# Projections by token tiles, and five token groups in front of the experts: one change to a fused encoder kernel

## The reference

```python
h  = patches(x) @ W.T + b + pos                       # 36 rows a sequence
ht = gelu(tok_embed[x_txt] @ W1.T + b1) @ W2.T + b2   # 32 rows a sequence
h  = concatenate([h, ht], axis=1)
y  = layernorm(h) @ fq_weight(w_qkv).T + b_qkv        # then fq_act: needs min and max of all of y
attn = int_log_softmax(fq_act(q @ k.T * hd**-0.5)); o = fq_act(attn @ v)
h  = h + fq_act(o @ fq_weight(w_proj).T + b_proj)
x2 = layernorm(h)
scores = sigmoid(x2 @ router_w.T); idx = top_k(scores + balance_bias, 2)
h  = h + mlp_shared(x2) + sum over the 2 experts of weight * mlp_expert(x2)   # mlp: square(relu(x@w1))@w2, 8 experts
```

## Time and profile before

| what | us |
|---|---|
| median of 3 runs | 1002.32 |
| the profiled execution's own time | 1000.82 |
| its span, first to last instruction | 999.0 |
| TensorE busy / VectorE busy | 623.0 / 724.1 |
| ScalarE busy / GpSimd busy | 512.8 / 325.4 |
| mean granted TensorE clock, share of full | 0.694 |

### The profile page before, as it was taken

The page is one execution under the profiler, slowest core; times in us unless marked ns, Lnnn a source line. Parts: engine busy times, 40 slices in busy tenths (PEclk is TensorE's granted clock), DMA queues, the critical chain, the costliest instruction groups (busy, mean ns, idle before and its releaser), DMA issues.

```text
span 999.0 us, 20044 instructions
## 1 busy us (share of the span) xinstructions
PE 623.0 (62%) x6502; PEld 472.7 (47%) x6502; DVE 724.1 (72%) x1719; ACT 512.8 (51%) x898; POOL 325.4 (33%) x347
## 2 busy tenths in 40 slices
PE   3599688586543377604888888734222357998950
PEld 2599577475432244402555555423122246776740
DVE  3435554767577599967999999999888754657773
ACT  3122276453531844233888888843644225887820
POOL 2022355444333121001232222220046770025575
PEclk9999698897867555555556555555555587999985
DMA  7963044221101344302222222272111323567653
GB/s 182 255 178 100 12 121 120 58 59 40 59 21 39 81 109 116 85 0 52 33 42 42 45 42 41 26 221 89 52 44 67 127 88 85 154 176 219 188 141 103
DMA packets 155152, 92.76 MB, mean 93 GB/s; under 512 B 88488, under 2 KB 147696, under 8 KB 154960
## 3 DMA queue, kind: packets, MB, share of 16 engines
q1 hardware_dynamic: 147232, 72.28, 28.0%
q0 software_dynamic: 7856, 19.68, 6.8%
HBM read 45.62 MB, written 31.85 MB: 78 GB/s over the span
## 4 chain that ended last, share of the span: by engine, by line
DVE 22%; PE 21%; issue 18%; SPq 15%; POOL 14%; ACT 5%; DMA 4%; POOLq 1%; DVEq 0%; ACTq 0%
PE ps L1702 16%; SPq L591 7%; POOL x_by_expert L752 5%; POOL R L761 3%; ACT R L768 3%; POOL R L695 2%; DVE M L1285 2%; DVE M L1286 2%; SPq L566 2%; SPq L565 2%; SPq L567 2%; POOL R L686 1%; PE ps L1969 1%; POOL R L684 1%; DVE R L1275 1%
## 5 line engine op out<-in xcount | busy, mean ns | idle before, releaser
L1702 PE MATMUL ps<-R 128*128 128x256 f16 (+6 forms) x2024 | 304.6, 307 | 48.2 <-DVE R L1659 12.9
L1702 PEld LDWEIGHTS ps<-R 128*128 128x128 f16 (+3 forms) x2024 | 222.5, 132 | 102.1 <-issue 52.4
L768 ACT ACTIVATE R<-ps 128x768 f16<-128x768 f16 (+7 forms) x257 | 178.1, 730 | 101.6 <-PE ps L1969 36.0
L1702 PE MATMUL ps<-M 32*128 32x68 bf16 (+4 forms) x1192 | 101.6, 245 | 101.7 <-DMA M<-R 69.4
L1702 PEld LDWEIGHTS ps<-M 32*128 32x128 bf16 (+3 forms) x1192 | 65.7, 116 | 153.7 <-issue 61.2
L771 ACT ACTIVATE R<-R,sc 128x512 f16<-128x512 f32 (+11 forms) x107 | 83.8, 839 | 101.9 <-DMA R<-v_rows 28.0
L768 ACT ACTIVATE R<-R 128x512 f16<-128x512 f32 (+5 forms) x145 | 74.7, 533 | 105.8 <-POOL R L686 66.6
L733 POOL TENSOR_TENSOR R<-R,M 128x884 f32<-128x884 f32 x32 | 53.2, 1664 | 147.7 <-ACT M L912 147.7
L761 POOL DMA_INDIRECT R<-y_by_tile,M x68 | 67.0, 986 | 101.0 <-DMA y_by_tile<-R 82.1
L752 POOL DMA_INDIRECT x_by_expert<-R,M x68 | 67.2, 988 | 59.7 <-DVEq L1578 39.5
L1873 PE MATMUL ps<-ident_b,R 128*68 128x128 bf16 x416 | 56.2, 308 | 20.9 <-ACT R L768 19.0
(11 more groups left out here) (279 smaller groups left out, 1130.9 us busy)
## 6 DMA issues: line engine op xcount, KB each, us to landing
R<-x_by_expert SPq DMA_DIRECT2D x41, 192.0 KB, 2.9
y_by_tile<-R SPq DMA_DIRECT2D x41, 192.0 KB, 2.6
R<-in_x_dram SPq DMA_DIRECT2D x12, 576.0 KB, 8.4
M<-R SPq DMA_DIRECT2D x16, 260.0 KB, 3.1
M<-R SPq DMA_DIRECT2D x32, 130.0 KB, 2.0
R<-w_split SPq DMA_DIRECT2D x1, 4032.0 KB, 22.7
v_rows<-R SPq DMA_DIRECT2D x16, 204.0 KB
R<-v_rows SPq DMA_DIRECT2D x16, 204.0 KB
```

Of the source, the lines that this page charges most:

```text
L768: return act.activation(out_, in_, ACT.Copy)
L1702: return pe.matmul(o, a, b, start=start, stop=stop, skip_group_check=True)
```

## The change

**Projection.** The columns of `xT` are ordered by tile, so `x_out` writes them one behind the other. `qkv` takes units of tiles instead of sequences: 8 of text (2 tiles, 256 columns) and 8 of images (3 tiles, 288 columns), at the steps of `UNITS_AT`: text units at 2 to 7, 24 and 26, image units at 10, 11, 16, 17, 22, 23, 25 and 28. There are 30 steps. `evac_qk` and `extremes_qkv` of an image unit reach into the sequence order by runs of 3 values with steps of 6, and `evac_qk` reads the bank with a step of 96 values. Normalising moves to ScalarE (`normal`, one instruction), the bias of V becomes one more matmul with three rows for each tile (`ones_three`, `bv_three`, prepared by `v_ratio`), the maximum of V is taken while it is scaled, all three channels of `by_patch` are on GpSimd, six buffers instead of four hold normalised tiles, and `turn_x` follows one step behind `x_low`.

**V.** The 16 loads become 4 of 816 KB, issued by ScalarE ahead of `to_halves`.

**Experts.** Five groups; `READY` becomes 11, 19, 29, 37, 41. ScalarE normalises (two Identity instructions for a pair) in `x2_high`. Square roots become Ln and Exp, the sigmoid an Exp with an addition and a reciprocal on VectorE. `weigh` (the weights of the copies) is split from `choose` and put later. 12 shared units stand ahead of the routed ones. `combine` is spaced by 2 steps.

```diff
-WINDOWS = [(0, 5), (5, 12), (12, 17)]
-SHARED_FIRST = 10
+WINDOWS = [(0, 2), (2, 6), (6, 11), (11, 15), (15, 17)]
+SHARED_FIRST = 12
-        XSTEP = [k // 2 for k in range(16)] + [6 * q + 8 + w // 2 for q in range(3) for w in range(6)] + [23, 23, 24, 26, 26, 26]
-        GSTEP = [11, 12, 14, 15, 17, 18, 20, 21, 23, 24, 25, 26, 27, 28, 29, 30]
+        XSTEP = [k // 2 for k in range(16)] + [6 * q + 8 + w // 3 for q in range(3) for w in range(6)] + [23, 23, 23, 26, 26, 26]
+        UNITS_AT = {2: 0, 3: 1, 4: 2, 5: 3, 6: 4, 7: 5, 10: 8, 11: 9, 16: 10, 17: 11, 22: 12, 23: 13, 24: 6, 25: 14, 26: 7, 28: 15}
-        WSTEP = [6, 7, 13, 16, 19, 22]
+        WSTEP = [9, 12, 13, 18, 19, 21]
...
-                pool.tensor_tensor(v, h, mv[0:n, x, 0:1].to_broadcast([n, C]), ALU.subtract).then_inc(sem("centred"), 1)
-                pool.tensor_tensor(v, v, rs[0:n, 2, x:x + 1].to_broadcast([n, C]), ALU.mult).then_inc(sem("xn"), 1)
-                pool.tensor_tensor(v, v, bvrow[0:N, :].unsqueeze(1).to_broadcast([N, 4, C]), ALU.add).then_inc(sem("v_stored"), 1)
+                ident_(xf1[0:n, x % XR1], h, scale=rs[0:n, 2, x:x + 1], bias=rs[0:n, 0, x:x + 1]).then_inc(sem("xn"), 1)
...
-                    copy(to, o.rearrange("p (k b h) -> p k b h", k=3, h=GRID)).then_inc(sem("xT"), 1)
+                copy(xT[:, :, x_cols(x)], ps[:, 4, :].bitcast(F16)[:, at:at + 3 * n].rearrange("p (k t) -> p k t", k=3)).then_inc(sem("xT"), 1)
...
+                        y = y[:, 16 * q:16 * q + 16, 0:NI].rearrange("p b (h w) -> p b h w", w=GRID)[:, :, :, 3 * half:3 * half + 3]
+                        o = o[:, 0:288].rearrange("p (w b h) -> p b h w", w=3, h=GRID)
...
             barrier(act, "act")
+            for q in range(4):
+                act.dma_start(yv[:, 16 * q:16 * q + 16, :], v_dram[16 * q:16 * q + 16].rearrange("b n c -> n b c")).then_inc(sem("v_in"), 16)
-            act.wait_ge(sem("v_in"), 16 * 16)
+            act.wait_ge(sem("v_in"), 16 * 4)
...
-                act.activation(rs2[:, 1, t], rs2[:, 0, t], ACT.Sqrt).then_inc(sem("ln2_sqrt"), 1)
+                chain(act, "scalar_step", act.activation(rs2[:, 1, t], rs2[:, 0, t], ACT.Ln))
+                act.activation(rs2[:, 1, t], rs2[:, 1, t], ACT.Exp, scale=0.5).then_inc(sem("ln2_sqrt"), 1)
...
+                act.wait_ge(sem("ln2_done"), window_of(i) + 1)
+                wait(act, "rows2", i - 1)
+                for j in range(2):
+                    n = 2 * i + j
+                    last = ident_(xf[:, i % 2, j, :], hf[:, n, :], scale=rs2[:, 2, n:n + 1], bias=rs2[:, 0, n:n + 1])
+                chain(act, "scalar_step", last)
...
-                        if s > GSTEP[0]:
-                            extremes_qkv(GSTEP.index(s) - 1)
-                        scale_v(GSTEP.index(s))
+                if s - 1 in UNITS_AT:
+                    extremes_qkv(UNIT_ORDER.index(UNITS_AT[s - 1]))
+                if s in UNITS_AT:
+                    scale_v(UNIT_ORDER.index(UNITS_AT[s]))
...
+                        mm(o, both, wqT1[:, 2 * C:3 * C], False, False)
+                        last = mm(o, ones_three[:, 0:m], bv_three, False, True)
...
+            def beside(low, more):
+                for k in range(max(len(low), len(more))):
+                    if k < len(more):
+                        residual(more[k])
+                    if k < len(low):
+                        x2_low(low[k])
+                    if k < len(more):
+                        stats(more[k])
...
+            beside([], [0, 1])
             variances(0)
             deviations(0)
+            beside([0, 1], [2, 3])
             choose(0)
+            beside([], [4])
             place(0)
+            beside([], [5])
             variances(1)
             deviations(1)
+            beside([2, 3, 4, 5], [6, 7, 8])
             choose(1)
...
+            beside([15, 16], [])
+            weigh(2)
+            weigh(3)
+            choose(4)
+            place(4)
             make_table()
+            weigh(4)
             y_rows()
```

More of the change, by code:

```diff
@@ L969, in x2_out, with exponentials @@
                      ps[:, 4 + i % 2, :].bitcast(F16)[:, 0:6 * P].rearrange("p (k t) -> p k t", k=3)).then_inc(sem("X"), 1)
-            def sigmoids(w):
+            def exponentials(w):
                 t = WBLK[w]
                 act.wait_ge(sem("routed"), WINDOWS[w][1])
-                act.activation(scores[:, t, :], ps[:, 6, t.start * E:t.stop * E].rearrange("p (i e) -> p i e", e=E), ACT.Sigmoid, scale=s1(W_RU)).then_inc(sem("sigmoid"), 1)
-            def x2_window(w):
-                first, end = WINDOWS[w]
-                for i in range(first, end + 1):
-                    if i < end:
-                        x2_high(i)
-                    if i > first:
-                        x2_out(i - 1)
@@ L984, in _ @@
-            for i in range(8):
+                act.activation(scores[:, t, :], ps[:, 6, t.start * E:t.stop * E].rearrange("p (i e) -> p i e", e=E), ACT.Exp, scale=s1(W_RU)).then_inc(sem("sigmoid"), 1)
+            for i in range(5):
                 y_whole(i)
             roots(0)
+            x2_high(0)
+            x2_high(1)
+            x2_out(0)
+            y_whole(5)
+            x2_out(1)
+            exponentials(0)
+            y_whole(6)
+            y_whole(7)
+            roots(1)
@@ L987, in _ @@
+            x2_high(2)
             y_whole(8)
+            x2_high(3)
+            x2_out(2)
             y_whole(9)
-            x2_window(0)
-            sigmoids(0)
-            for i in range(10, 14):
-                y_whole(i)
-            roots(1)
-            y_whole(14)
+            x2_high(4)
+            x2_out(3)
+            x2_high(5)
+            x2_out(4)
+            x2_out(5)
+            exponentials(1)
+            for i in range(10, 13):
+                y_whole(i)
+            roots(2)
@@ L1225, in _ @@
             ln_deviation(0)
-            for s in range(STEPS):
+            ch(dve.memset(ext, 0.0))
+            for s in range(STEPS + 1):
                 if s >= 1 and s - 1 in LN_STEP:
@@ L1512, in deviations @@
                 ch(ts(rs2[:, 2, t], rs2[:, 2, t], X_UNIT, None, ALU.mult))
-            def normal(i):
-                wait(dve, "rows2", i - 1)
-                for j in range(2):
-                    n = 2 * i + j
-                    last = ts(xf[:, i % 2, j, :], hf[:, n, :], mv2[:, n, 0:1], rs2[:, 2, n:n + 1], ALU.subtract, ALU.mult)
-                last.then_inc(sem("xf"), 1)
+                ch(dve.scalar_tensor_tensor(rs2[:, 0, t], rs2[:, 2, t], -1.0, mv2[:, t, 0], ALU.mult, ALU.mult))
+                dve.drain().then_inc(sem("ln2_done"), 1)
             def x2_low(i):
@@ L1558, in choose, with weigh @@
                 tt(mask[:, t, :], at[:, :, 0, :], at[:, :, 1, :], ALU.add).then_inc(sem("mask"), 1)
+            def weigh(w):
+                t = WBLK[w]
+                n = t.stop - t.start
+                s, at, got = scores[:, t, :], chosen[:, t], picked[:, 0:n]
                 ch(tt(got, at, s.unsqueeze(2).to_broadcast([P, n, TOP, E]), ALU.mult))
@@ L1594, in make_table @@
                     ch(tt(cum[:, b, n:NQE], cum[:, a, n:NQE], cum[:, a, 0:NQE - n], ALU.add))
-                ends = cum[:, 1, :]
-                ch(dve.scalar_tensor_tensor(start_row, full[:, 0:3, :], float(TILE), own, ALU.mult, ALU.add))
+                ends = cum[:, 0, :]
+                ch(dve.scalar_tensor_tensor(start_row, full[:, 0:NW, :], float(TILE), own, ALU.mult, ALU.add))
                 ch(tt(tiles, ends, tiles, ALU.subtract))
@@ L1954, in turn_window @@
                         route(i - 2)
-            for w in range(3):
+            for w in range(NW):
                 turn_window(w)
```

424 lines of the change are left out of this document (242 added, 182 removed).

## The result

The changed kernel took 970.49 us (median of 4, 964.69 to 976.77) where before took 1001.39 beside it: ratio 0.969, interval 0.962 to 0.976. The forecast was 945, its range 921 to 983. The profiled execution has a span of 974.8 us, 24.2 less than before's 999.0 and 32 more than the sum. It was the slowest of the four (976.77), so its trace shows 24 of the 31 us that the medians show.

The account below looks back on a forecast made before the run. A ring of waits, with no engine full, was taken to bound the projection stage. From the span of 999.0, -52 (projection) -1.2 (V) +8.7 (prelude) -11.7 (tail) gave 942.8; with 1.8 outside the span, 945 us, range 921 to 983.

Parts of the forecast that it names:

- forecast case: Whole kernel: all terms come as summed, 945 us, own range 930 to 962; chance 0.55.
- The third case: Projection's evacuations and reductions: steps cost 3.6 ns a value everywhere, +28 us, time 973; chance 0.16.
- the fourth case: Projection: the ring closes again elsewhere, in ScalarE's in-order stream; the stage saves 25 instead of 52, time 972; chance 0.09.
- the V term: V's loads: issuing four costs ScalarE 5.5 us, VectorE's 6.65 us wait goes; -1.2 us, between -5.5 and +3.
- Projection, -52: Projection stage of 206.5 us: with the ring open it ends near 266 instead of 318 us, saving 52.
- The ring: Projection: GpSimd's normalising and V bias and VectorE's scaling and `x_low` wait in a circle; GpSimd waits 83.2 us for scaling.
- 13 in additions: Projection: 5 us for image evacuations and 8 us for parts at the low clock, on top of 141.4 for steps.
- The 5 us for the evacuations: Projection: evacuating an image unit's Q and K takes 0.9 us; about 5 us of the excess is in the way.
- Its own sign of being wrong: V's loads: the prediction would be wrong if ScalarE's issues of V took over 8 us.
- Prelude and shared units, +8.7: Experts: first routed tile comes 10.5 us later, behind 12 shared units, 1.8 comes back; +8.7, between +2 and +14.
- Tail, -11.7: First routed tile to end: third group starts two tiles sooner, 157.8 us instead of 169.5; between -4 and -14.
- The slower case: Projection: TensorE stays at 1.2 GHz, its 101 us become about 203, stage ends at 340, time 1019; chance 0.06.

Follow-up runs that it names:

- the four cases of GpSimd: Changed kernel, V's loads back on SyncE, with neither, normalising, V's bias or both back on GpSimd: ratios 0.9423, 0.938, 0.939, 0.9735.
- v_act_16: Changed kernel with V loaded by 16 DMAs from ScalarE at the same place instead of four of 816 KB: 1047.85 us, ratio 0.9716.
- v_on_sp: Changed kernel with V's loads put back as 16 DMAs of 204 KB issued by SyncE: 1017.18 us, ratio 0.9423.
- v_mid: Changed kernel with V's 16 loads on SyncE behind groups 0 to 13, two behind groups 6 and 10: 928.98 us, ratio 0.9292.

## Why the prediction was right in sign and off by half in size

The time of 970.49 us lies in the range of 921 to 983, but not in the forecast case's own 930 to 962. Near it stood only the third and the fourth case (973 and 972), for which the range had been widened, and neither happened. That the range held is luck: the miss came from the V term, which none of the cases had.

- **Projection, -52, measured -58.3, by itself -61.6.** The ring was the right diagnosis, shown by the four cases of GpSimd: it needs both pieces. But it was half of the gain, and the text spoke as if it were the whole. The stage's work ended at 263.1 (266 forecast), 151.6 us in place of 141.4 for the steps and 13 in additions. That the sum came so near is in part luck too. The 5 us for the evacuations had no ground (646 ns, not 0.9 us); what the low clock cost is not separated from the rest (granted 0.88, up from 0.81); and two steps of 8.8 and 8.9 us, where TensorE waits behind a batch of deviations, put in some 11 us that the sum didn't have. VectorE's work came to 112.9, the upper end. Another 3.5 us, not foreseen, are the scales: VectorE waited 4.1 us for GpSimd's reduction there, now 0.6.
- **The third case (steps cost 3.6 ns a value everywhere).** It did not happen. The rule of the Trainium skill ("Advanced Engine Details and Errata", section "Memory Cachelines") holds in this case for `x_out`, 1273 ns with steps of 12 bytes and 407 in order. Of its statement on the bank little shows here: a read with 384 bytes from value to value ran at 646 ns for 288, beside 576 for 256 and 583 for 272 in order. The prediction also misread its runs of 3 by that rule: with a step of 24 bytes from run to run, every second run has one value alone in its line. The reductions ran as in order all the same.
- **V, -1.2 between -5.5 and +3, measured +33.8: the failed step.** The prediction took 5.5 us for issuing four loads, and 8.5 as the upper end, from "0.47 for one large issue and 8.00 for the one behind it, blocked". It read the blocked 8.00 as one price for the whole set; it was the price behind each load. And it took it from a load of 128 partitions, which all 16 engines carry, for loads of 68, which four carry: 0.27 against 1.02 of the engines, 48 us instead of some 10. The row was the nearest at hand, and it differed in what mattered. (The bound of +3 is not what its working gives either: 8.5 less 6.7 is 1.8.) Its own sign of being wrong, issues of V at over 8 us, came out at 34.8. The 16 issues of before took 0.3 us each though such loads are as slow in transfer (0.27 of the engines in `v_act_16`), since they stood 5 us apart with other work between them. In place of the step stand 34.8 us of issue and 7.3 us of late Q and K, less 6.65 and 1.7 us of VectorE's waits that went: 33.8. Undone, it gives back 34.0.
- **Prelude and shared units, +8.7, measured +12.3 and +1.0 ahead of it.** The working held to 1.6 us at every scatter. The first routed tile is 2 us later than the sum (818.25; 839.75 - 23.6 = 816). The 1.8 us that the prediction gave back for before's start on cold tiles lie behind that tile (its second comes 4.35 us later before, 2.27 after), so the two rows are better held against +10.5 and -13.5 than against +8.7 and -11.7.
- **Tail, -11.7, measured -13.0** (156.6 us; 157.8 forecast). Right also in its mechanism: the third group's gathers begin 94 us behind the first routed tile and run through.
- **The slower case and the fourth** did not happen: the clock rose, and ScalarE waited at most 14 us for any one line. The slower case was also priced a little high: 101 us by its own rows (4.05 against 2.12) become 193, not 203.

## What to carry to other kernels

In these runs an issue of a DMA was cheap (0.3 to 0.8 us) with nothing large ahead of it, and cost up to 13.5 us behind a slow load: price it by the transfer ahead of it, and read the share of the DMA engines, which shows when a load leaves most of them idle (0.27 for 68 partitions, 1.02 for 128). Such loads belong between other work, not in a block on a queue that the path needs. A ring of waits can need two edges in one stream: try each alone before crediting either, and ask how much of the gain the ring holds. Where a stage is opened, sum the fullest engine's work by steps, and in the steps with a batch of small operations on another engine ask who waits for them: that was the 11 us which the sum lacked.

## Not expected

The queue's price does not depend on the engine (ScalarE 34.8 us, SyncE 46 with the fourth load's), and a single load of 3264 KB costs its issuer 0.52 us. What V would cost as two loads, of 64 and of 4 partitions, was not tried. On the first chip (`v_on_sp`) VectorE's chained small operations at the end of the prelude stood 1.40 us apart:

```profile
780.76 0.20 DVE L1697 TENSOR_TENSOR R<-R 128x40 f32<-128x40 f32 x1 [1.20 <-DVE R L1696]
782.16 0.20 DVE L1698 SCALAR_TENSOR_TENSOR R<-R 128x40 f32<-128x40 f32 x1 [1.20 <-DVE R L1697]
```

where in `v_mid`, on the third, their kind stand 0.2 to 0.3 apart (735.62, 735.86 and 736.08 for three of 40 values). Other gaps in that stage end with "issue" or "remote", on ScalarE up to 13.6 us. Why that chip is slow just there is open. A prelude with more small operations would suffer most by it, and the experts' part was 0.6% slower on the second chip and neither slower nor faster on the third. That this is the reason is not shown.
